# A last feed-forward whose gate and up products are made from polynomial moments, with its down weights built during the linear attention

## What is computed

```python
w = 0.5 * (2.0 * p1 + (p2 - p0) * f + (2.0 * p0 - 5.0 * p1 + 4.0 * p2 - p3) * f2
           + (3.0 * p1 - p0 - 3.0 * p2 + p3) * f3)
...
gate_w = spline_reconstruct(gate_cp, INTER, HIDDEN)      # 2048 x 512
up_w = spline_reconstruct(up_cp, INTER, HIDDEN)
down_w = spline_reconstruct(down_cp, HIDDEN, INTER)      # 512 x 2048
gate = jnp.einsum('bsh,ih->bsi', hidden_states, gate_w)
up = jnp.einsum('bsh,ih->bsi', hidden_states, up_w)
inter = jax.nn.silu(gate) * up
return jnp.einsum('bsi,hi->bsh', inter, down_w)
```

## Time and profile before

| | before |
|---|---|
| median of 3 runs | 2404.9 us (2403.79 to 2405.71) |
| profiled execution, its own time | 2401.79 us |
| its span in the trace | 2400.0 us |
| TensorE (PE) busy | 2245.5 us, 94% |
| VectorE (DVE) busy | 1133.1 us, 47% |
| ScalarE (ACT) busy | 866.2 us, 36% |
| GpSimd (POOL) busy | 175.4 us, 7% |

### The profile page before, as it was taken

One profiled execution on the slowest core, in us unless ns is written; L12 is line 12 of the kernel. 1 busy time (PEld: TensorE's weight loads), 2 busy tenths in 40 slices (PEclk: granted clock), 3 DMA queues, 4 the chain that ended last, 5 costly groups with the idle time before them and its releaser, 6 DMA issues.

```text
span 2400.0 us, 25795 instructions
## 1 busy us (share of the span) xinstructions
PE 2245.5 (94%) x9444; PEld 1246.9 (52%) x9444; DVE 1133.1 (47%) x2367; ACT 866.2 (36%) x1697; POOL 175.4 (7%) x356
## 2 busy tenths in 40 slices
PE   8999999999998989999999999968877888799999
PEld 3555554556664445555555556634434555444444
DVE  1433434474223855556555557755445666411111
ACT  1323332312221644545454445533333555311111
POOL 0000100000000211111101001000000000000000
PEclk9999999998999999999999999989988999999999
DMA  5444443334523311100000122010020111000000
GB/s 221 169 142 183 174 170 139 155 126 138 185 79 110 130 42 58 59 24 23 20 26 20 32 78 96 14 35 19 10 85 13 52 52 59 12 1 9 5 9 9
DMA packets 52513, 178.88 MB, mean 75 GB/s; under 512 B 5457, under 2 KB 25233, under 8 KB 46590
## 3 DMA queue, kind: packets, MB, share of 16 engines
q1 hardware_dynamic: 50662, 139.49, 16.9%
q0 software_dynamic: 1728, 37.75, 4.1%
HBM read 121.58 MB, written 46.47 MB: 70 GB/s over the span
## 4 chain that ended last, share of the span: by engine, by line
PE 81%; DVE 11%; ACT 4%; issue 2%; DMA 1%; SPq 0%; POOL 0%; DVEq 0%; ACTq 0%; POOLq 0%
PE psum L119 64%; PE psum L112 7%; PE psum L1468 5%; PE psum L1513 4%; DVE small L2300 2%; ACT WK L2258 1%; PE psum L1056 1%; DVE R L1223 1%; PE psum L2227 1%; DVE R L1222 1%; DVE R L1794 1%; DMA R<-in_wkv 1%; DVE WK L251 0%; DVE small L228 0%; DVE WK L1213 0%
## 5 line engine op out<-in xcount | busy, mean ns | idle before, releaser
L119 PE MATMUL psum<-R,WK 128*125 128x512 f32 (+7 forms) x3536 | 1325.2, 523 | 28.4 <-DMA WK<-in_ctxT 7.4
L119 PEld LDWEIGHTS psum<-R,WK 128*112 128x112 f32 (+4 forms) x3536 | 594.6, 174 | 687.3 <-issue 566.8
L112 PE MATMUL psum<-small,WK 112*125 112x112 f32 (+5 forms) x2036 | 280.7, 267 | 90.3 <-ACT WK L2264 28.5
L112 PEld LDWEIGHTS psum<-small,WK 112*125 112x125 f32 (+5 forms) x2036 | 228.7, 154 | 192.9 <-issue 92.5
L119 PE MATMUL psum<-WK,R 128*112 128x375 f32 (+3 forms) x704 | 221.0, 453 | 10.5 <-DVE R L1794 7.0
L1644 DVE TENSOR_REDUCE small<-psum 112x1 f32<-112x487 f32 x128 | 85.0, 664 | 194.4 <-PE psum L119 191.2
L119 PE MATMUL psum<-R 128*128 128x112 f32 (+3 forms) x960 | 158.7, 309 | 17.4 <-DVE R L1794 16.2
L119 PEld LDWEIGHTS psum<-WK,R 128*112 128x112 f32 (+2 forms) x704 | 111.8, 171 | 84.7 <-issue 14.8
L119 PEld LDWEIGHTS psum<-R 128*128 128x128 f32 (+3 forms) x960 | 116.1, 184 | 56.2 <-issue 26.2
L1468 PE MATMUL psum<-R,WK 128*112 128x512 f32 x256 | 120.1, 592 | 0.0
L1563 ACT ACTIVATE WK<-psum,small 112x487 f32<-112x487 f32 x128 | 97.0, 758 | 54.1 <-DVE small L1646 53.1
(11 more groups left out here) (214 smaller groups left out, 2126.7 us busy)
## 6 DMA issues: line engine op xcount, KB each, us to landing
R<-in_wf POOLq DMA_DIRECT2D x6, 4096.0 KB, 14.1
d_w<-R POOLq DMA_DIRECT2D x6, 2048.0 KB, 18.6
R<-d_w SPq DMA_DIRECT2D x6, 2048.0 KB, 11.2
WK<-in_ctxT SPq DMA_DIRECT2D x16, 750.0 KB, 5.6
d_v<-WK SPq DMA_DIRECT2D x16, 750.0 KB
R<-in_wq SPq DMA_DIRECT2D x7, 1024.0 KB, 7.3
R<-in_wo SPq DMA_DIRECT2D x6, 1024.0 KB, 17.1
d_k<-X SPq DMA_DIRECT2D x8, 750.0 KB, 3.2
```

The lines of the kernel that those rows point to most:

```text
L112: ins = pe.transpose(dst, src, idn[0:k, 0:k])
L119: ins = pe.matmul(dst, lhs, rhs, start=k == 0, stop=k == len(pairs) - 1)
```

## The change

Gate and up are no longer made dense. For each token, each of the four 128-wide parts of `xn` is reduced to moments: its sums against 1, q, q^2 and q^3, over the whole part and over what lies right of each of 7 possible knot places, 4 + 7*4 = 32 features. Four parts give 128 features. The 2048 rows of gate and up are sorted by where their knots fall, into 21 windows of 61 to 109 rows (`spline_windows`) of which each needs only 7 knot places per part. For a window, 4 products with 32-column weights (`features`) fill the four quarters of a PSUM bank's partitions; ScalarE or VectorE copies them (`fT`); one product of `fT` with the window's columns of coefficients (`columns`, gate and up side by side) gives both. `Silu` replaces the copy, the Tanh and the extra multiplication. The hidden units now stand in the windows' order, so the down weights' rows are put in that order too.

The preparation: `attention0` turns and stores only the down coefficients; the gate and up coefficients are stored once as rows (`d_feat`). `load_rows` fetches these in the windows' order, 125 DMAs in SP's queue ahead of `back`. `attention2` builds the down weights alone, 48 units in its first six turns; VectorE prepares rows and features in turns 3 to 7 and 9 (`prepare`), and 42 transposes with 11 ScalarE copies turn the rows to columns in the last three turns (`turn_rows`, `keep_columns`). SP stores the down weights to DRAM (`store_down`, 4 MB) and loads them back in the new order in seven parts, 161 DMAs, behind the key and value loads of `attention3` (`turn_down`). `ternary_layer` has no units left.

```diff
+    def load_rows(sp):
+        for v, (_, _, _, blocks) in enumerate(windows):
+            for at, f, width, high in blocks:
+                src = bass.AP(tensor=d_feat.tensor, offset=f * 68, ap=[[243 * 68, high], [35 * 68, width], [1, 68]])
+                sp.dma_start(taken[at:at + width * high, v].rearrange("p k e -> p (k e)"), src
+                             ).then_inc(sem("spline_taken"), 16)
...
     def pe(pe, u):
+        if u >= len(units):
+            return
         k, t = units[u]
         if u == 0:
-            pe.wait_ge(sem("spline_cgu"), 16)
-        if (k, t) == (16, None):
             pe.wait_ge(sem("spline_cd"), 16)
...
+                    for k in range(4 * (i - 8), 4 * (i - 7)):
+                        spline["turn_rows"](pe, k)
...
-                    if i < NB:
-                        for u in range(3):
-                            spline["pe"](pe, 88 + 5 * i + u)
...
+                    if b:
+                        spline["turn_down"](sp, b - 1)
...
+                def gate_up(b, k):
+                    if k == 0:
+                        for q in range(quads):
+                            (dve_ring if q % 2 else act_ring).wait_drained(pe, b, f"f{q}")
+                    dve_ring.wait_free(pe, b, f"u{k}")
+                    for v in FILLS[k]:
+                        at, count = windows[v][0], windows[v][1]
+                        to = 256 * (v % 2)
+                        ins = product(pe, dve_ring.bank[f"u{k}"][:, to:to + 2 * count],
+                                      [(fT[:, v, :], columns[:, 2 * at:2 * (at + count)])])
+                    ins.then_inc(dve_ring.sem_filled, 1)
+
+                def feature(b, q):
+                    ring = dve_ring if q % 2 else act_ring
+                    ring.wait_free(pe, b, f"f{q}")
+                    for v in range(4 * q, min(4 * q + 4, NV)):
+                        for kt in range(KT):
+                            ins = product(pe, ring.bank[f"f{q}"][kt * NFEAT:(kt + 1) * NFEAT, (v % 4) * P:(v % 4 + 1) * P],
+                                          [(features[:, v, kt, :], xnT[:, kt, :])])
+                    ins.then_inc(ring.sem_filled, 1)
...
+                    for c, part in enumerate((range(0), range(0, 3), range(3, 6), range(6, pairs))):
                         if b2 is not None:
-                            dve_ring.wait_drained(pe, b2, f"u{FC - 1}")
-                            act_ring.wait_free(pe, b2, f"h{c}")
-                            transposes(pe, [(act_ring.bank[f"h{c}"][:, j * P:(j + 1) * P],
-                                             h[:, (4 * c + j) * P:(4 * c + j + 1) * P]) for j in range(4)], ident
-                                       ).then_inc(act_ring.sem_filled, 1)
+                            turn_h(b2, c)
+                        if b1 is not None:
+                            for k in part:
+                                gate_up(b1, k)
...
+                    for q, part in enumerate((range(0, 6), range(6, 8), range(8, 10), range(10, FT))):
+                        if b2 is not None:
+                            down(b2, part)
+                        if b0 is not None and q < 3:
+                            if q == 0:
+                                act_ring.wait_drained(pe, b0, "xnT")
+                            for k in range(2 * q, 2 * q + 2):
+                                feature(b0, k)
```

More of the change, by code:

```diff
@@ L1714, in spline_weights @@
             side = A.get(2 * 4 * P, dt=BF16, i=2, t=4, q=P)
-            units = []
-            for k in range(32):
-                units.append((k, None))
-                units += [(k, t) for t in range(4 if k < 16 else 2)]
+            units = [(k, t) for k in range(16) for t in (None, 0, 1)]
             pieces_upto = []
@@ L1777, in act @@
                     if k >= 2:
-                        last = max(v for v in range(len(units)) if units[v][0] == k - 2)
-                        act.wait_ge(sem("spline_second"), pieces_upto[last])
+                        act.wait_ge(sem("spline_second"), 2 * (k - 1))
                     ins = act.activation(side[:, k % 2].rearrange("p t c -> p (t c)"), place(u), ACT.Relu)
@@ new lines, in prepare @@
+            def prepare(dve, i):
+                link = dve_chain.on(dve)
+                if i == 3:
+                    which(dve, link)
+                if 4 <= i < 8:
+                    for e in range(4 * (i - 4), min(4 * (i - 3), 14)):
+                        ins = row_of(dve, e // NPOS, e % NPOS)
+                    if i == 7:
+                        ins.then_inc(sem("spline_rows"), 1)
+                        dve.wait_ge(sem("spline_rows"), 1)
+                if i == 9:
+                    moments(dve, link)
@@ new lines, in turn_rows @@
+            def turn_rows(pe, k):
+                if not 0 <= k < len(FILLS):
+                    return
+                if k == 0:
+                    pe.wait_ge(sem("spline_rows"), 1)
+                    pe.wait_ge(sem("spline_second"), pieces_upto[-1])
+                if k >= 2:
+                    pe.wait_ge(sem("spline_columns"), k - 1)
+                first = windows[FILLS[k][0]][0]
+                for v in FILLS[k]:
+                    at, count = 2 * (windows[v][0] - first), windows[v][1]
+                    ins = transposes(pe, [(place(k)[:, at + w * count:at + (w + 1) * count],
+                                           rows[0:count, v, w].rearrange("p k e -> p (k e)")) for w in range(2)], ident)
+                ins.then_inc(sem("spline_turned_rows"), 1)
@@ new lines, in keep_columns, with whole @@
+            def keep_columns(act, k):
+                if not 0 <= k < len(FILLS):
+                    return
+                act.wait_ge(sem("spline_turned_rows"), k + 1)
+                first, last = windows[FILLS[k][0]], windows[FILLS[k][-1]]
+                n = 2 * (last[0] + last[1] - first[0])
+                act.copy(columns[:, 2 * first[0]:2 * first[0] + n], place(k)[:, 0:n]).then_inc(sem("spline_columns"), 1)
+            def whole(pe):
+                pe.wait_ge(sem("spline_columns"), len(FILLS))
+                pe.wait_ge(sem("spline_features"), 1)
@@ L1801, in attention2 @@
+            turned_count = sum(len(list(row_pieces(v))) for v in range(NV))
+            return dict(turned_count=turned_count, load_rows=load_rows, load=load, store_down=store_down, turn_down=turn_down, pe=pe, act=act, dve=dve,
+                        places=places, prepare=prepare, turn_rows=turn_rows, keep_columns=keep_columns, whole=whole)
         def attention2(stage, n):
@@ new lines, in down @@
+                def down(b, part):
+                    if part[0] == 0:
+                        dve_ring.wait_free(pe, b, "y")
+                    for ft in part:
+                        if ft % 4 == 0:
+                            act_ring.wait_drained(pe, b, f"h{ft // 4}")
+                        ins = pe.matmul(dve_ring.bank["y"][:, :], hT[:, ft, :], turned_wd[:, ft, :], start=ft == 0,
+                                        stop=ft == FT - 1)
+                    if part[-1] == FT - 1:
+                        ins.then_inc(dve_ring.sem_filled, 1)
```

345 lines of the change are left out of this document (239 added, 106 removed).

## The result

The changed kernel takes **2274.08 us** (median of 4 runs, 2269.61 to 2274.46), the kernel before 2404.35 (4 runs, 2403.79 to 2405.71). The ratio is 0.9453, 95% interval 0.9437 to 0.947: 5.5% less. So the spans differ by 132.2 us and the medians by 130.3; 2285 had been forecast.

The account below looks back on a forecast made before the run. TensorE was taken to bound `spline_ffn`, waits `ternary_layer` and `attention3`. Last feed-forward -103, linear attention +2.7, layer -15 and first attention -5.5 sum to -120.8 from 2404.9, so 2285 us; range 2262 to 2330.

Parts of the forecast that it names:

- SP's queue: Loads in `attention3`: free below 1.26 us each; rival: slower from about 2.1 us, near 2285 + 290, chance 0.03.
- the layer: `ternary_layer`: without units, a chain of product, addition, norm and transposes remains, 5.4 us a tile; -15 us.
- I allow 1.0 us a tile: Waits in `spline_ffn`: allowance for window pairs going through three banks, judged just covered; part of 29.5 us a tile.
- the table's last line: From the first product of `spline_ffn` to the end: predicted -103 us, with turns of 29.5 instead of 43.9 us.
- The price of a pair: Window pair in `spline_ffn`: 1.9 us with hand-overs, for three banks 0.64 a pair against 0.65 of TensorE.
- The rest of the linear attention: Linear attention after its start: turns without units save 7.2 and 4.4 us, row transposes +1.6, VectorE +1.
- `attention3`, "unchanged": `attention3`: would stay at 31.4 us a tile, change 0; late keys there would mean SP.
- The early load: Start of the linear attention: TensorE's first unit now waits for the load of `d_cd`, +11.7 us.
- the first attention: First attention: 80 fewer transposes, -4.5 us, and a shorter coefficient copy and store at its end, -1; together -5.5 us.
- Two quarters or little more: Rival, `spline_ffn`: features overlap over only two quarters, 8.9 instead of 5.0 us a tile, +27 us, 2312; chance 0.17.
- One after another: Rival, `spline_ffn`: feature products do not overlap, 18.0 instead of 5.0 us a tile, +91 us, 2376; chance 0.06.
- ScalarE paces the windows: Rival, `spline_ffn`: small Silu cost 0.6 us each, +6 a tile, 2327; chance 0.11, shared with several thin covers.

## Why the prediction was right, by its steps

**The mechanisms held one by one**: four quarters at once, 109 ns for four records, 30 ns a record with the start of a burst; the whole wait for `d_cd`; the chain of the layer at 5.41 us a tile, where 5.4 had been said; the small engines beside TensorE; SP's queue at no cost (the 125 row loads took 64.6 us and the first `back` was issued at 1493.50 instead of 1481.94, and TensorE waited for neither). The forecast missed by 11 of 130 us, and these terms of the sum were mis-sized:

- **"I allow 1.0 us a tile"** for waits in `spline_ffn`. It measured nothing: the turn took 28.47 instead of 29.5. The rest of that sum held: features and the entering and leaving of bursts, 5.7 there, came to 5.6, of which 0.6 stands in the down products (14.3 instead of 13.7). Five full turns at 1.03 us less make 5.2 of the 6.2 us by which the table's last line beats the forecast; the rest lies at the stage's ends. The price of a pair (1.9 us, from copies and products of other sizes) was a little high. Silu of 97 columns took 250 ns and its multiplication 253; two banks instead of three give about 1.7 for the whole pair. By its own sum three banks just covered, and the allowance was put on top of that.
- **"The rest of the linear attention"**, -12.1 instead of -9.0, in three parts. The five turns with units took 79.06 instead of 79.64, -0.6, where +1 had been allowed for VectorE's new work: the first two went 1.6 us faster, the next two 1.4 slower, and what VectorE's work did in them can't be told. The next two turns, without units, gave -4.3, where -4.8 was said; the second of them, from 1703.35 to the next `q` product at 1717.31, is 13.96, where 13.7 was said. What follows took 28.4 instead of 35.6, -7.2, where -5.2 was said (-2.4, -4.4 and +1.6); 0.9 of it is the last product, which took 3.69 instead of 4.62.
- **`attention3`, "unchanged"**: its middle is, with keys 156.6 us from the third tile's issue to the last one's in both kernels. Of the 2.5 us 1.1 lie ahead of it, where over the first 36 us the granted clock was 0.81 in this execution and 0.76 in that of before. 1.0 lies in the 15 us from 1999.4, with the clock at 1.00, where before had 0.89 from 2021.0, and 0.4 in the stage's end. In four of the experiments that leave this stage alone the clock of the first 36 us was 0.76 three times and 0.86 once, and the stage came out up to 5 us longer than in the changed kernel's profile. So it differs from run to run and not by the change, and it is most likely why the profiled execution lies 4.5 below its median.
- The early load, the first attention and the layer are within 1 us of the forecast.

**The rivals.** *Two quarters or little more* was priced by 0.053 us a record (+27 us). The mechanism was not what the kernel did, and the price was wrong as well: with two quarters in turn the kernel needed 8.2 us more, not 27, since the next two quarters began before these were through. *One after another* was put at +91; made as strictly as the banks allow, it cost 73, and 39 with runs of eight. Both prices assumed that no record is issued past a quarter that is busy; by the reading above three can wait for it. *ScalarE paces the windows* (0.6 us a Silu) fell with the 250 ns. *SP's queue* had its mechanism right, and its two bounds stand beside what four times the issues did: 88 to 100 issues at 0.46 us are as if each of 22 to 25 loads cost 1.8, between the 1.26 from which it was to cost something and the 2.1 from which it was to make the kernel slower; it cost 39 us and left the kernel faster than before.

The Trainium skill ("TensorE: Matmul & The Clock Gate", Part 3, on packing small matmuls) gives 2.38x for three column tiles. Here four went at 168 records in 5.0 us, against 18.0 one after another: 3.6x, entering and leaving the bursts included. So the trace does better than an estimate by that figure, for one tile more.

## What to carry to other kernels

Where small products can be written to different quarters of the output's partitions, let neighbours in the program name different ones: the same instructions took 5.0 us a tile with four in turn, 6.5 with two, 11.1 with runs of eight to one and 15.0 with runs of 16. When work that used to fill the start of a stage is replaced by work with a late operand, price the wait at the whole of what stands behind it, and look for a place in memory that is free early: here an area and one moved issue gave back 14 us, more than 10% of what the change had won. And when a chain is cut, work out the next one before naming the gain: behind the norm stood the one bank, and behind the bank the next stage's first norm.

## What the runs showed of the chip that was not expected

- TensorE issues records past a busy quarter: at a change of quarter the new one starts while three records of the old one are still to come (467 ns between chains of eight, where eight in a row take 872). By the same reading, with two quarters in turn it started two new ones while three of each old one were to come. No row of before showed it, and it took 52 us off the price of the wrong order (39.5 instead of 91).
- A chain of records to one quarter keeps 109 ns for 128 columns, its first step of 133 to 134 aside, whatever the other quarters do; four chains side by side did not slow each other down.
- Issues on SP's queue for scattered row loads cost 0.45 to 0.51 us in `attention3`, and 0.83 in the first part, where they stand behind the loads of weights, keys and values (23 issues in 19.19 us from 1751.80).
